# A transformer kernel on one core: setup ahead of the branch, mask passes over half their columns, and a new order of stages

## The chip, the core and the metric

The kernel runs on one core of a Trainium2 chip. Its engines are PE (matrix products; PEld is its weight load), DVE (vector), ACT (activations), POOL (general) and SP, which here only issues DMAs. Each engine runs its own list of instructions in order and waits on semaphores that the others raise. The metric is the device time of one execution in microseconds (us). Matmul results go to PSUM banks, which the program calls Q0 to Q3, HID0, HID1, Y0 and Y1.

## The reference

```python
# x: (32, 512, 256) f32; all matrices f32
x = x + linear_attention(layernorm(x))   # causal, 16 heads of 16, phi(v) = elu(v) + 1, out by W_out
x = x + ffn(layernorm(x))                # relu(h @ tern(W1).T + b1) @ tern(W2).T + b2, 256 -> 1024 -> 256
x = x + window_attention(layernorm(x))   # 16 query heads, 4 key heads, RMS-normed q and k, rotary, gain,
                                         # window of 64 keys, pairs of heads mixed, out by Wo
x = x + ffn(layernorm(x))
# tern(W) = clip(round(W / (mean|W| + 1e-5)), -1, 1)
```

Every one of the 32 sequences goes through all four parts; only the weights are shared.

## The kernel before

The products that need more than one pass's precision are split into a high and a low part (names in `_h`, `_l`, `hi`, `lo`), and each product is then three passes, or two for the FFN, whose weights are -1, 0 or 1.

**Steps.** `steps` runs 34 steps in software pipelining. `phase1` of a step works on the linear attention of sequence a, `phase2` on the window attention of the sequence before it, b. The eight blocks `up(0)` to `up(7)` and `down(0)` to `down(7)` of the FFNs are spread between the attention's stages, so that PE has work while DVE and ACT prepare the attention's next operands. Step numbers 2 to 30 are a hardware loop; the others are written out. The order of the stages is a list of calls written by hand, one list for each engine and phase: for instance, PE's `turn_q(t)` waits for DVE's `stack_lo(t)`, and DVE's `low(k)` for ACT's `relu(k)`.

**First phase**, on four chunks of 128 tokens: `qk`, `values` (projections), `phi` and `by_parity` on DVE (feature map; two copies of q with every second head zero), `turn_keys`, `state` (PE sums k v per chunk into Q2, DVE's `state` writes the running sum to SBUF, and PE's next `state` waits for that), `scores`, `mask` (DVE multiplies by the causal table), `numer`, `turn_numer`, `normalise`, `turn_y`, `y_hi`, `y_lo`, `project`, `residual`.

**Second phase**, on four tiles of 128 tokens: `sums` (sums of squares), `root_step(group, n)` (ten small dependent steps of an inverse root; group 0 is tile 0, group 1 tiles 1 to 3), `cosines`, POOL's `sines`, `rotate`, `norm_qk`, ACT's `stack_hi`, DVE's `stack_lo`, then `turn_q`, `turn_k` and their evacuation by ACT, `scores(t)`, ACT's `exps(t)`, `numer`, `turn_numer`, `normalise`, `turn_y`, `project`, `residual`. `own_apply` and `own_norm` are the layernorm of the next FFN, `next_stats`, `next_apply`, `next_norm` that of the next attention, whose input DMA SP issues after the store that waits for `finish_second`.

**Masks of the window attention.** `scores(t)` first writes the mask into the score banks: a matmul of 32 rows, of `qodd_rows` (or `qfirst_rows`) as weights and the one-hot table `hot` as moving operand, adds -1e30 where a key may not be seen. The table is one-hot over 64 queries, so it takes two passes, m = 0 and 1, each with 32 queries' rows, and each runs over the columns of all 64 queries. The four row groups g run side by side on the array. A score matmul then adds q k.

**Setup.** `both_ways` reads one flag and branches to one of two copies of the program; with these inputs the copy without guarding maxima runs. Everything that follows it, the setup of the weights too, stands inside the copies. SP alone has no branch. DVE's `prepare_rest` mixes Wo, sums |W1| and |W2| (`gsum`, then PE's `sum_rows`, then the thresholds `thr`), makes the low parts of three weights and some tables; POOL's `quantise` turns W1 and W2 into their ternary form from `thr` on.

Of the kernel before, what the change touches and what calls it, by code (L numbers as in the profile page):

```python
# [19 lines left out]
ALU = mybir.AluOpType  # L20
# [6 lines left out]
P = 128  # L27
# [68 lines left out]
def build(nc, x, w_qkv, w_out, w_b, wo_b, gain, mix, w1, b1, w2, b2, const, out):  # L96
    with ExitStack() as ctx:
# [164 lines left out]
        class Step:  # L262
# [3 lines left out]
            def __init__(self, i):  # L266
# [3 lines left out]
                self.last = isinstance(i, int) and i == NSEQ + 1  # L270

# [33 lines left out]
        def _(sp):  # L305
            sp.dma_start(gains[:, 0:H], gain.partition_broadcast(P)).then_inc(gain_in, 16)
            sp.dma_start(st_a[:, 0:KB * 3 * D].rearrange("p (k n) -> p k n", k=KB),
                         w_qkv.rearrange("(k p) n -> p k n", p=P)).then_inc(loaded_first, 16)
            sp.dma_start(cst[:], const).then_inc(loaded_first, 16)

# [7 lines left out]
            load(0)  # L318
            sp.wait_ge(x_in, 16)
# [44 lines left out]
        def _(pe):  # L364
# [163 lines left out]
            def program(guarded):  # L528
                def phase1(s):
# [137 lines left out]
                    down(4)  # L667
                    qk(a, 2)
                    values(0)
                    up(6)  # L670
                    qk(a, 3)
                    down(5)
                    up(7)
                    turn_keys(0)
                    values(1)
# [4 lines left out]
                    scores(0)  # L680
                    state(1)
                    down(7)
                    up(0)
                    numer(0, 0)
                    state(2)
                    numer(0, 1)
                    up(1)
                    turn_numer(0)
                    bias()
                    scores(1)  # L690
                    up(2)
                    turn_y(0)
# [15 lines left out]
                    up(3)  # L708
                    turn_y(2)
                    down(2)  # L710
# [8 lines left out]
                    project(3)  # L719
                    qkv(s.b, 2, a + 1)  # L720
                    down(3)
                    qkv(s.b, 3, a + 1)

                def phase2(s):
# [63 lines left out]
                    def mask(bl, g, m, blocks=1):  # L788
                        n, at_col = blocks * REP, bl % 2 * REP * W
                        table = qodd_rows if bl else qfirst_rows  # L790
                        pe.matmul(B_SCORES[g][:, at_col:at_col + n * W].rearrange("p (u q) -> p u q", u=n),  # L791
                                  table[rows_of(g), m, :], hot[rows_of(g), m, :].unsqueeze(1).broadcast_to([BR, n, W]),
# [105 lines left out]
                    own_norm(0)  # L898
                    turn_q(1)
                    turn_numer(0)  # L900
# [14 lines left out]
                    down(0)  # L915
                    turn_y(1)
                    up(2)
                    project(1)
                    turn_q(3)
                    turn_k(3)  # L920
                    numer(2)
                    down(1)
                    next_norm(0)
                    scores(3)
                    turn_numer(2)
                    next_norm(1)
                    down(2)
                    turn_y(2)
                    numer(3)
                    qk(s.next_a, 0, b)  # L930
                    project(2)
                    up(3)
# [978 lines left out]
```

## Time and profile before

| | |
|---|---|
| median of 3 executions | 2942.03 us |
| lowest and highest | 2939.92 and 2947.65 us |
| the profiled execution | 2938.5 us, of which 2936.7 us span |
| mean granted TensorE clock | 0.99 |
| PE, DVE, ACT, POOL busy | 94%, 78%, 59%, 17% |

The span runs from the first to the last instruction of the program. "Busy" is the time in which an engine has an instruction in it; matmuls overlap, and each shows its own latency too, so the distance of two starts tells the pace, and not the duration. A bracket behind a row of the timeline tells how long the engine was idle before it and what ended that. A row of the timeline or chain with x4 merges four instructions.

### The profile page before, as it was taken

To read this page: it belongs to the slowest core of one execution; us is meant where nothing else is said; L and a number is where in the kernel's file an instruction comes from. 1 tells how busy PE (TensorE), PEld (TensorE's weight loads), DVE (VectorE), ACT (ScalarE), POOL (GpSimd) and SP (SyncE) were. 2 spreads that over 40 slices of the span, in tenths; PEclk is the share of its full clock that TensorE was granted. 3 is DMA by queue.
4 is the path that set the end of the run, shared out by engine and by line. 5 is a ranking of instruction groups with operands and counts; after the bars stand their busy time and mean duration, and the time that the engine had idled before them with its cause. 6 is when DMAs were issued, how large, how long until landed. Compare 5 with 4: busy or idle time off the path is not lost.

```text
span 2936.7 us, 75526 instructions
## 1 busy us (share of the span) xinstructions
PE 2765.1 (94%) x25924; PEld 2241.4 (76%) x25924; DVE 2290.2 (78%) x5983; ACT 1744.2 (59%) x3589; POOL 486.6 (17%) x1047
## 2 busy tenths in 40 slices
PE   5799999999999999999999999999999999999986
PEld 3677777877778877778877778877778877778865
DVE  6677888787888787888787888787888787888754
ACT  2356665566665566665566665566665566665554
POOL 5111111111111111111111111111111111111110
PEclk9999999999999999999999999999999999999998
DMA  2000000000000000000000000000000000000000
GB/s 71 8 11 18 17 17 3 14 17 17 17 17 3 14 17 17 17 17 3 14 17 17 17 17 3 14 17 17 17 17 3 14 17 17 17 17 3 16 11 18
DMA packets 42050, 45.04 MB, mean 15 GB/s; under 512 B 2640, under 2 KB 41360, under 8 KB 42000
## 3 DMA queue, kind: packets, MB, share of 16 engines
q1 hardware_dynamic: 42000, 44.40, 4.8%
q8 instruction: 28, 0.46, 0.1%
q14 instruction: 22, 0.18, 0.0%
HBM read 21.32 MB, written 16.78 MB: 13 GB/s over the span
## 4 chain that ended last, share of the span: by engine, by line
PE 72%; DVE 14%; issue 7%; ACT 6%; DMA 1%; DVEq 1%; SPq 0%; POOL 0%; ACTq 0%; POOLq 0%
PE Q L380 18%; PE HID L440 13%; PE Y L464 12%; PE Q L621 5%; PE Q L594 4%; ACT a_qz L1164 4%; PE HID L388 3%; PE Q L854 2%; PE Q L644 2%; PE Q L609 2%; PE Q L791 2%; PE Q L797 2%; PE Q L867 1%; PE Q L651 1%; DVE b_ss L1564 1%
## 5 line engine op out<-in xcount | busy, mean ns | idle before, releaser
L983 ACT ACTIVATE f_r<-HID,b1c 128x512 f32<-128x512 f32 x512 | 358.3, 700 | 454.7 <-PE HID L440 433.7
L464 PE MATMUL Y<-w2t,f_hh 128*128 128x256 f32 x2048 | 539.7, 296 | 7.8 <-DVE f_hl L1328 7.8
L464 PE MATMUL Y<-w2t,f_hl 128*128 128x256 f32 x2048 | 510.9, 282 | 0.0
L440 PE MATMUL HID<-ff_xh,w1t 128*128 128x512 f32 x1024 | 433.5, 423 | 17.5 <-ACT f_hh L984 15.4
L1328 DVE TENSOR_TENSOR f_hl<-f_r,f_hh 128x512 fp32r<-128x512 f32 x512 | 351.8, 687 | 104.3 <-ACT f_hh L984 101.3
L464 PEld LDWEIGHTS Y<-w2t,f_hh 128*128 128x128 f32 x2048 | 388.8, 190 | 38.0 <-DVE f_hl L1328 13.8
L440 PE MATMUL HID<-ff_xl,w1t 128*128 128x512 f32 x1024 | 407.3, 398 | 0.0
L464 PEld LDWEIGHTS Y<-w2t,f_hl 128*128 128x128 f32 x2048 | 390.0, 190 | 6.9
L984 ACT ACTIVATE f_hh<-HID,b1c 128x512 fp32r<-128x512 f32 x512 | 356.9, 697 | 0.0
L440 PEld LDWEIGHTS HID<-ff_xh,w1t 128*128 128x128 f32 x1024 | 193.7, 189 | 99.7 <-ACT f_hh L984 44.5
L1434 DVE TENSOR_TENSOR a_s<-Q,cst 128x512 f32<-128x512 f32 x384 | 246.3, 683 | 27.8 <-PE Q L594 27.7
L1164 ACT ACTIVATE a_qz<-Q 128x512 f32<-128x512 f32 x384 | 201.7, 600 | 76.0 <-PE Q L797 76.0
L440 PEld LDWEIGHTS HID<-ff_xl,w1t 128*128 128x128 f32 x1024 | 194.6, 190 | 24.1
L1841 POOL TENSOR_TENSOR a_s<-a_s,cst 128x160 f32<-128x160 f32 x128 | 64.5, 504 | 788.4 <-ACT a_s L1019 697.6
L1820 POOL TENSOR_SCALAR at_tmp<-at_mv 128x4 f32<-128x4 f32 x64 | 20.8, 326 | 945.6 <-DVE at_mv L1306 945.6
L1072 ACT ACTIVATE a_relu<-Q 128x512 f32<-128x512 f32 x128 | 76.6, 598 | 164.8 <-PE Q L621 164.8
L594 PE MATMUL Q<-a_qz,a_kT 32*128 32x256 f32 x1536 | 152.9, 398 | 1.8 <-DVE a_qz L1425 1.8
L1320 DVE TENSOR_TENSOR at_xl<-HID,at_xh 128x512 fp32r<-128x512 f32 x122 | 84.1, 689 | 90.2 <-ACT at_xh L968 90.2
L1078 ACT ACTIVATE a_yh<-Q 128x256 fp32r<-128x256 f32 x128 | 49.2, 384 | 173.0 <-PE Q L651 173.0
L621 PE MATMUL Q<-a_s,a_v 128*32 128x128 f32 x4096 | 145.5, 276 | 3.1 <-DVE a_s L1434 3.1
L594 PE MATMUL HID<-a_qz,a_kT 32*128 32x256 f32 x512 | 145.0, 402 | 0.0
L621 PEld LDWEIGHTS Q<-a_s,a_v 128*32 128x32 f32 x4096 | 100.2, 109 | 34.0 <-issue 10.9
(197 smaller groups left out, 7366.9 us busy)
## 6 DMA issues: line engine op xcount, KB each, us to landing
x<-in_x SPq DMA_DIRECT2D x32, 512.0 KB, 4.1
out<-x SPq DMA_DIRECT2D x32, 512.0 KB, 3.0
b_vm<-b_v SPq DMA_DIRECT2D x64, 96.0 KB, 2.1
x<-in_w SPq DMA_DIRECT2D x2, 512.0 KB, 4.5
a_s<-in_w_qkv SPq DMA_DIRECT2D x1, 768.0 KB, 5.2
cst<-in_const SPq DMA_DIRECT2D x1, 645.0 KB, 6.3
ff_xn<-in_w SPq DMA_DIRECT2D x1, 512.0 KB, 6.5
f_r<-in_w SPq DMA_DIRECT2D x1, 512.0 KB, 6.8
```

Source lines behind the costliest of these rows:

```text
L380: mm = pe.matmul(dst, a, b, start=(start and k == 0 and j == 0), stop=(last and k == n - 1 and j == 2), skip_group_check=loose)
L388: mm = pe.transpose(bank[:, k * D + t * P:k * D + (t + 1) * P], n.xn[:, 2 * hf + t, k * P:(k + 1) * P], ident)
L440: mm = pe.matmul(banks[fb % 2][:], w1t[:, k, fb * P:(fb + 1) * P], src[:, k, :], start=(k == 0 and j == 0), stop=(k == KB - 1 and j == 1))
L464: mm = pe.matmul(Y[t // 2][:, (t % 2) * D:(t % 2 + 1) * D], h[:, fb % 2, t * P:(t + 1) * P], w2t[:, fb, :], start=False, stop=(fb == FB - ...
L594: mm = pe.matmul(A_SCORES[r][:, k * 2 * P:(k + 1) * 2 * P].rearrange("p (e q) -> p e q", e=2), a_kT[rows, k, ch * P:(ch + 1) * P], a_qz[ro ...
L621: mm = pe.matmul(Q[3][VW * j:VW * (j + 1), cols], a_v[:, ch, k * HB + 2 * r + e, :], a_s[:, ch % 2, r, j * P:(j + 1) * P], start=(r == 0), ...
L983: act.activation(f_r[:, fb % 2, :], banks[fb % 2][:], ACT.Relu, bias=b1c[:, fb:fb + 1]).then_inc(f_rr, 1)
L984: act.activation(f_hh[:, fb % 2, :], banks[fb % 2][:], ACT.Relu, bias=b1c[:, fb:fb + 1]).then_inc(f_act, 1)
L1164: act.activation(b_p[:, g, :], B_SCORES[g][:, :], ACT.Exp).then_inc(b_ex, 1)
L1320: dve.tensor_tensor(n.xl[:, :, hf * D:(hf + 1) * D], banks[hf][:, :].rearrange("p (k n) -> p k n", k=KB), n.xh[:, :, hf * D:(hf + 1) * D], ...
L1328: dve.tensor_tensor(f_hl[:, fb % 2, :], f_r[:, fb % 2, :], f_hh[:, fb % 2, :], ALU.subtract).then_inc(f_lo, 1)
L1434: dve.tensor_tensor(a_s[:, ch % 2, r, :].rearrange("p (h q) -> p h q", h=4), A_SCORES[r][:, :].rearrange("p (h q) -> p h q", h=4), causal. ...
```

## The change

Four things change together.

- SP loads x ahead of the constants and the weights of the projection. ACT's rounding of those weights (`round_first`), DVE's first statistics and layernorm, and POOL's first `norm_rstd` stand ahead of `both_ways`.
- DVE's `prepare_rest` is taken apart into `mix_weights`, `weight_sums(j)`, `low_weights`, `thresholds` and `small_tables`. The first two (`weight_sums` for W1) stay ahead of the steps, the others stand between the stages of step 0's first phase; PE's `sum_rows` moves there too.
- A mask pass m writes only the columns of its own 32 queries: half as many columns in each matmul, and as many matmuls as before.
- Stages of both phases stand in another order on PE, ACT and DVE.

The diff, with indentation taken off; lines of "..." stand for unchanged code.

```diff
+    self.first = isinstance(i, int) and i == 0
 def first_turn(s):
...
     sp.dma_start(gains[:, 0:H], gain.partition_broadcast(P)).then_inc(gain_in, 16)
-    sp.dma_start(st_a[:, 0:KB * 3 * D].rearrange("p (k n) -> p k n", k=KB),
-                 w_qkv.rearrange("(k p) n -> p k n", p=P)).then_inc(loaded_first, 16)
-    sp.dma_start(cst[:], const).then_inc(loaded_first, 16)
-
     def load(a):
         if needed(a * NT):
         sp.dma_start(x0[:], src.rearrange("(t p) d -> p t d", p=P)).then_inc(x_in, 16)
     load(0)
+    sp.dma_start(cst[:], const).then_inc(loaded_first, 16)
+    sp.dma_start(st_a[:, 0:KB * 3 * D].rearrange("p (k n) -> p k n", k=KB),
+                 w_qkv.rearrange("(k p) n -> p k n", p=P)).then_inc(loaded_first, 16)
     sp.wait_ge(x_in, 16)
     for half in range(KB):
         sp.dma_start(st_ffn[0][half], w1[half * P:(half + 1) * P]).then_inc(loaded, 16)
...
     up(5)
-    down(4)
     qk(a, 2)
     values(0)
     up(6)
+    down(4)
     qk(a, 3)
     down(5)
     up(7)
+    values(1)
     turn_keys(0)
-    values(1)
+    if s.first:
+        sum_rows()
     own_norm()
     turn_keys(1)
     down(6)
     state(0)
     scores(0)
+    up(0)
     state(1)
     down(7)
-    up(0)
+    state(2)
     numer(0, 0)
-    state(2)
     numer(0, 1)
     up(1)
     turn_numer(0)
+    scores(1)
     bias()
-    scores(1)
+    turn_y(0)
     up(2)
-    turn_y(0)
     down(0)
     project(0)
...
     up(3)
+    down(2)
     turn_y(2)
-    down(2)
     numer(3, 0)
     numer(3, 1)
     project(2)
     turn_y(3)
     qkv(s.b, 1, a + 1)
     project(3)
+    down(3)
     qkv(s.b, 2, a + 1)
-    down(3)
     qkv(s.b, 3, a + 1)
 def phase2(s):
...
         n, at_col = blocks * REP, bl % 2 * REP * W
         table = qodd_rows if bl else qfirst_rows
-        pe.matmul(B_SCORES[g][:, at_col:at_col + n * W].rearrange("p (u q) -> p u q", u=n),
-                  table[rows_of(g), m, :], hot[rows_of(g), m, :].unsqueeze(1).broadcast_to([BR, n, W]),
+        mine = slice(BR * m, BR * m + BR)
+        pe.matmul(B_SCORES[g][:, at_col:at_col + n * W].rearrange("p (u q) -> p u q", u=n)[:, :, mine],
+                  table[rows_of(g), m, :], hot[rows_of(g), m, mine].unsqueeze(1).broadcast_to([BR, n, BR]),
                   start=(m == 0 and (guarded or bl % 2 == 0)), stop=False, skip_group_check=True)
...
     own_norm(0)
+    turn_numer(0)
     turn_q(1)
-    turn_numer(0)
     down(7)
     turn_k(1)
     own_norm(1)
     turn_numer(1)
     scores(2)
     down(0)
+    up(2)
     turn_y(1)
-    up(2)
-    project(1)
     turn_q(3)
-    turn_k(3)
     numer(2)
     down(1)
+    turn_k(3)
+    project(1)
     next_norm(0)
     scores(3)
+    down(2)
+    next_norm(1)
     turn_numer(2)
-    next_norm(1)
-    down(2)
+    numer(3)
     turn_y(2)
-    numer(3)
     qk(s.next_a, 0, b)
     project(2)
     up(3)
...
 qk(0, 0)
 qk(0, 1)
-sum_rows()
 steps(pe, phase1, phase2)
 both_ways(pe, program)
...
     qk_exp(2)
+    relu(6)
     values(0)
-    relu(6)
     qk_exp(3)
     relu(7)
+    values(1)
     keys(0)
-    values(1)
     own_norm()
     keys(1)
     relu(0)
...
     own_norm(0)
+    evacuate_q(1)
     stack_hi(2)
-    evacuate_q(1)
     evacuate_k(1)
     own_norm(1)
     y_hi(0)
...
     relu(1)
+    exps(2)
     y_hi(1)
-    exps(2)
     relu(2)
+    evacuate_numer(2)
     evacuate_q(3)
     evacuate_k(3)
-    evacuate_numer(2)
     next_norm(0)
     exps(3)
     next_norm(1)
...
-        round_first()
-        norm_hi(at, 0, Q)
         round_rest()
         steps(act, phase1, phase2)
+    round_first()
+    norm_hi(at, 0, Q)
     both_ways(act, program)
...
                       ALU.subtract).then_inc(prepared, 1)
-def prepare_rest():
+def mix_weights():
     dve.wait_ge(loaded, 16 * N_LOADS)
     for i in range(2):
         dve.tensor_scalar(mixed[:, i, :], st_wo[:, 0, :], mixc[:, i:i + 1], None, ALU.mult).then_inc(setup, 1)
-    dve.tensor_copy(b2h[:], b2f[:]).then_inc(prepared, 1)
     dve.wait_ge(setup, 4)
     for i in range(2):
         dve.scalar_tensor_tensor(out=mixed[:, i, :], in0=st_wo[:, 1, :], scalar=mixc[:, 2 + i:3 + i],
                                  in1=mixed[:, i, :], op0=ALU.mult, op1=ALU.add).then_inc(setup, 1)
-    for j in range(2):
-        for half in range(2):
-            dve.tensor_reduce(gsum[:, 2 * j + half:2 * j + half + 1], st_ffn[j][half], X, ALU.add,
-                              apply_absolute_value=True).then_inc(abs_sums, 1)
+
+def weight_sums(j):
+
+    dve.wait_ge(loaded, 16 * N_LOADS)
+    for half in range(2):
+        dve.tensor_reduce(gsum[:, 2 * j + half:2 * j + half + 1], st_ffn[j][half], X, ALU.add,
+                          apply_absolute_value=True).then_inc(abs_sums, 1)
+
+def low_weights():
+
     dve.wait_ge(rounded, 4)
     for hi, lo, src in ((wout_h, wout_l, st_a[:, KB * 3 * D:KB * 4 * D].rearrange("p (k n) -> p k n", k=KB)),
                         (wb_h, wb_l, st_wb.rearrange("p (k n) -> p k n", k=KB)), (wob_h, wob_l, mixed)):
         dve.tensor_tensor(lo[:], src, hi[:], ALU.subtract).then_inc(prepared, 1)
+    dve.wait_ge(prepared, 5)
+
+def thresholds():
+
+    dve.wait_ge(setup_pe, 1)
+    dve.tensor_scalar(thr[:, 0:2], Y[0][:, 0:2], 1.0 / (FF * D), Q_EPS, ALU.mult, ALU.add).then_inc(setup, 1)
+    dve.wait_ge(setup, 7)
+    dve.tensor_scalar(thr[:, 2:4], thr[:, 0:2], -0.5, None, ALU.mult).then_inc(setup, 1)
+    dve.wait_ge(setup, 8)
+    dve.tensor_scalar(thr[:, 0:2], thr[:, 0:2], 0.5, None, ALU.mult).then_inc(thr_set, 1)
+
+def small_tables():
+
+    dve.wait_ge(ones_set, 5)
+    dve.tensor_copy(b2h[:], b2f[:]).then_inc(prepared, 1)
     dve.wait_ge(prepared, 6)
     dve.tensor_tensor(b2f[:], b2f[:], b2h[:], ALU.subtract).then_inc(prepared, 1)
     dve.wait_ge(prepared, 7)
...
                              in1=b2f[:].unsqueeze(1).broadcast_to([2 * BR, 2, D]),
                              op0=ALU.mult, op1=ALU.add).then_inc(prepared, 1)
-    dve.wait_ge(setup_pe, 1)
-    dve.tensor_scalar(thr[:, 0:2], Y[0][:, 0:2], 1.0 / (FF * D), Q_EPS, ALU.mult, ALU.add).then_inc(setup, 1)
-    dve.wait_ge(setup, 7)
-    dve.tensor_scalar(thr[:, 2:4], thr[:, 0:2], -0.5, None, ALU.mult).then_inc(setup, 1)
-    dve.wait_ge(setup, 8)
-    dve.tensor_scalar(thr[:, 0:2], thr[:, 0:2], 0.5, None, ALU.mult).then_inc(thr_set, 1)
-
-    dve.wait_ge(ones_set, 5)
     dve.tensor_copy(ident_b[:], ident).then_inc(prepared, 1)
     dve.tensor_copy(ident_r[:], ident).then_inc(prepared, 1)
...
     low(5)
     phi(1)
+    if s.first:
+        weight_sums(1)
+    own_apply()
     phi(2)
-    own_apply()
     low(6)
     phi(3)
     by_parity(0)
+    by_parity(1)
+    if s.first:
+        thresholds()
+        low_weights()
     low(7)
-    by_parity(1)
     own_norm_lo()
     state(0)
     mask(0)
+    if s.first:
+        small_tables()
     state(1)
     finish_first(s)
     state(2)
     next_stats()
+    normalise(0)
     low(0)
-    normalise(0)
     mask(1, (0, 1))
     y_lo(0)
     mask(1, (2, 3))
     residual(0)
+    low(1)
     next_apply()
-    low(1)
     normalise(1)
     mask(2, (0, 1))
     y_lo(1)
     mask(2, (2, 3))
     next_norm_lo(0)
     residual(1)
+    f1_stats(0)
     low(2)
     next_norm_lo(1)
     normalise(2)
     mask(3, (0, 1))
     mask(3, (2, 3))
     y_lo(2)
-    f1_stats(0)
+    low(3)
     f1_stats(1)
     residual(2)
-    low(3)
     normalise(3)
+    f1_stats(2)
+    y_lo(3)
     low(4)
-    y_lo(3)
-    f1_stats(2)
     residual(3)
     f1_stats(3)
...
         return
     sums(0)
-    cosines(0)
+    sums(1)
     root_step(0, 0)
     root_step(0, 1)
-    sums(1)
+    cosines(0)
     root_step(0, 2)
     root_step(0, 3)
     root_step(0, 4)
-    rotate(0)
+    sums(2)
     root_step(0, 5)
     root_step(0, 6)
+    sums(3)
     root_step(0, 7)
+    rotate(0)
     root_step(0, 8)
+    root_step(1, 0)
     root_step(0, 9)
+    root_step(1, 1)
     norm_qk(0)
-    sums(2)
+    root_step(1, 2)
     low(5)
     stack_lo(0)
-    sums(3)
-    root_step(1, 0)
-    root_step(1, 1)
-    root_step(1, 2)
     root_step(1, 3)
-    low(6)
     root_step(1, 4)
     cosines(1)
     if guarded:
         maxima(0)
     root_step(1, 5)
-    rotate(1)
+    low(6)
     root_step(1, 6)
     root_step(1, 7)
+    cosines(2)
     root_step(1, 8)
     if guarded:
         maxima(1)
-    cosines(2)
+    own_apply()
+    rotate(1)
     root_step(1, 9)
+    norm_qk(1)
     rotate(2)
-    norm_qk(1)
-    own_apply()
+    low(7)
     stack_lo(1)
-    low(7)
     norm_qk(2)
     own_norm_lo(0)
     normalise(0)
...
     own_norm_lo(1)
+    y_lo(0)
     stack_lo(2)
-    y_lo(0)
     cosines(3)
     rotate(3)
+    residual(0)
     norm_qk(3)
-    residual(0)
     low(0)
     next_stats()
     if guarded:
         maxima(4)
         maxima(5)
     normalise(1)
-    y_lo(1)
     stack_lo(3)
     low(1)
+    y_lo(1)
     next_apply()
     if guarded:
         maxima(6)
...
             next_norm_lo(1)
+            y_lo(2)
             f2_stats(0)
-            y_lo(2)
             residual(2)
             normalise(3)
+            low(3)
             f2_stats(1)
-            low(3)
             y_lo(3)
-            low(4)
             residual(3)
             f2_stats(2)
+            low(4)
             f2_stats(3)
-        dve.wait_ge(x_in, 16)
-        norm_stats(at, 0, x0, range(NT))
-        prepare_first()
-        norm_apply(at, 0, x0)
-        norm_lo(at, 0, Q)
-        prepare_rest()
+        mix_weights()
+        weight_sums(0)
         steps(dve, phase1, phase2)
+    dve.wait_ge(x_in, 16)
+    norm_stats(at, 0, x0, range(NT))
+    prepare_first()
+    norm_apply(at, 0, x0)
+    norm_lo(at, 0, Q)
     both_ways(dve, program)
...
             second_rstd()
-        norm_rstd(at, 0)
         quantise()
         steps(pool, phase1, phase2)
+    norm_rstd(at, 0)
     both_ways(pool, program)
```

## Rows read from the trace of the kernel before

**Rows 1.** The profile's page: busy time, share of the span and instructions of each engine

```profile
PE 2765.1 (94%) x25924; PEld 2241.4 (76%) x25924; DVE 2290.2 (78%) x5983; ACT 1744.2 (59%) x3589; POOL 486.6 (17%) x1047
```

**Rows 2.** Timeline of SP's DMA issues: start, duration (us), line, transfer

```profile
516.41 0.39 SPq L316 DMA_DIRECT2D x<-in_x  x1
604.51 0.40 SPq L316 DMA_DIRECT2D x<-in_x  x1
```

**Rows 3.** Busy time by stretch of one iteration: us, PE, PEld, DVE, ACT, POOL, clock

```profile
461.90:498.00 36.10, 35.97 (x378) 29.62 (x377) 31.06 (x78) 16.40 (x33) 3.51 (x9) 1.00 0.00 0
498.00:512.30 14.30, 12.11 (x112) 9.65 (x110) 13.62 (x45) 10.54 (x24) 5.08 (x12) 1.00 0.06 14
512.30:549.90 37.60, 37.34 (x324) 30.30 (x325) 26.14 (x66) 27.34 (x56) 5.55 (x12) 1.00 0.08 28
```

**Rows 4.** Waits of PE in that iteration (us in total, times, longest)

```profile
PE Q L754 <- DVE b_ks L1630: 1.3, 2, 0.7
PE HID L440 <- ACT f_hh L984: 0.4, 1, 0.4
```

**Rows 5.** Timeline of PE: mask passes of 256 and of 512 columns, successors

```profile
506.34 0.28 PE L791 MATMUL Q<-hot,qfirst_rows 32*128 32x256 bf16 x3
506.46 0.27 PE L791 MATMUL Q<-hot,qodd_rows 32*128 32x256 bf16 x3
...
514.96 0.39 PE L791 MATMUL Q<-hot,qodd_rows 32*128 32x512 bf16 x3
515.19 0.38 PE L791 MATMUL Q<-hot,qodd_rows 32*128 32x512 bf16 x3
```

**Rows 6.** Timeline of PE: the transposes of 128 columns of turn_q(0), turn_k(0)

```profile
504.69 0.53 PE L754 MATMUL Q<-ident_r,b_qs 128*128 128x128 f32 x4 [0.71 <-DVE b_ks L1630]
505.06 0.33 PE L763 MATMUL Q<-ident_r,b_ks 128*128 128x128 f32 x2
```

**Rows 7.** Timeline of DVE, second phase, up to stack_lo(1)

```profile
498.70 0.49 DVE L1564 TENSOR_REDUCE b_ss<-a_eq 128x20 f32<-128x320 f32 x1
...
501.54 0.37 DVE L1592 TENSOR_TENSOR b_step<-b_step,b_var 128x20 f32<-128x20 f32 x1
...
504.36 0.28 DVE L1630 TENSOR_TENSOR b_ks<-a_s,b_ks 128x128 fp32r<-128x128 f32 x1
...
511.88 0.28 DVE L1630 TENSOR_TENSOR b_ks<-a_s,b_ks 128x128 fp32r<-128x128 f32 x1
```

**Rows 8.** Timeline of ACT, second phase: exps(0), relu(7); y_hi(1), exps(2)

```profile
507.52 1.57 ACT L1164 ACTIVATE a_qz<-Q 128x512 f32<-128x512 f32 x3 [1.38 <-PE Q L797]
...
510.02 0.72 ACT L984 ACTIVATE f_hh<-HID,b1c 128x512 fp32r<-128x512 f32 x1
...
523.72 0.38 ACT L1178 ACTIVATE a_yh<-Q 128x256 fp32r<-128x256 f32 x1 [1.46 <-PE Q L874]
524.00 1.57 ACT L1164 ACTIVATE a_qz<-Q 128x512 f32<-128x512 f32 x3
```

**Rows 9.** Timeline of PE, first phase: numer(0, 0), state(2), numer(0, 1)

```profile
470.18 0.65 PE L621 MATMUL Q<-a_s,a_v 128*32 128x128 f32 x16
470.75 0.73 PE L609 MATMUL Q<-a_v,a_kt 128*128 128x136 f32 x4
471.41 0.64 PE L621 MATMUL Q<-a_s,a_v 128*32 128x128 f32 x16
```

**Rows 10.** Chain that ended last, from the start: start, us, piece

```profile
2.16 7.50 DMA x<-in_x
...
15.01 7.06 DMA mixc<-in_mix
...
34.50 0.60 DVE a_kT L1418
...
47.73 0.42 DVE a_state L1444 x2
```

**Rows 11.** The branch of `both_ways`, line L298: duration in ns, start in us

```profile
L298 PEldq COMPARE_BRANCH  x1: 6322/6322/6322, 4.9 to 4.9; - x1
```

## The prediction

> **What bounds the kernel now.** I start at the page: PE is busy 94% of the span, DVE 78% [rows 1]. That is a mean over very different stretches, so the next view is the timeline of SP, whose load of x comes once in each iteration: two of them start 88.10 us apart [rows 2]. Some 31 such periods make up most of the 2936.7 us; a change of 0.1 us in an iteration is 3.1 us in the end.
>
> Inside one iteration the busy time by stretch separates three regimes [rows 3]. From 461.9 to 498.0 (first phase) PE is busy 35.97 of 36.10 us. From 498.0 to 512.3 (start of the second phase) PE has 12.11 of 14.30 us and DVE 13.62: here DVE sets the pace. From 512.3 to 549.9 PE has 37.34 of 37.60 us again. The waits agree: PE waits 1.3 us for `b_ks`, the end of `stack_lo`, in two waits (`turn_q(0)` and `turn_q(1)`), and 0.4 us once for `relu(5)` [rows 4]. Pauses under some 0.3 us between two stages don't show as idle time, since a matmul's own latency covers them; they show in the distance of starts.
>
> **Mask passes.** A pass of 512 columns starts 0.23 us before the next (514.96 to 515.19), and one of 256 columns 0.12 us (506.34 to 506.46) [rows 5]. Four row groups run together, so this is the price of the pass. After the change tiles 1 to 3 have passes of 256 columns: 3 tiles x 2 passes x (0.23 - 0.12) = 0.66 us. Tile 0 has four passes that fall to 128 columns, for which there is no row. From below: half of 0.12, which saves 4 x 0.06 = 0.24. From above, the nearest row: transposes of 128 columns, each with its weight load, start 0.37 / 4 = 0.09 us apart (504.69 to 505.06) [rows 6], which saves 4 x 0.03 = 0.12. I take 0.16, nearer to the transposes, since a weight load belongs to each mask pass too. Together 0.8 us an iteration (0.78 to 0.90), of PE's time. On the path it is less: what tile 0 saves lies ahead of `exps(0)` and ends in DVE's stretch, where I count it below. For tiles 1 to 3 I count 0.6 of 0.66.
>
> The 128-column passes are where a rule speaks against the change. The traces' transposes show a pass with its load every 0.09 us [rows 6]. The Trainium skill (TensorE: Matmul & The Clock Gate, LDWEIGHTS) says that a load takes its columns over 1.2 GHz, and that 32 rows cost as much as 128; an estimate from that page is 0.107 us a load, so that tile 0 would save next to nothing and the sum be 0.66. Row and rule differ by 0.16 us an iteration, 5 us in all; the forecast keeps its sign by either.
>
> **Second phase, DVE's stretch.** From the first `sums(0)` at 498.70 to the last instruction of `stack_lo(1)` at 511.88 DVE has no rest [rows 7]. (a) The new list puts `sums(3)` (0.4 us from start to start) and three steps of root group 1 (0.1 each, in gaps) ahead of `stack_lo(0)`. It gains by filling the gaps of dependent steps: `root_step(0, ...)` had starts 0.2 us apart where an independent successor comes after 0.1, and some six are now filled, 0.6 us. That is even, but POOL's `sines(2)` now starts later, beside the last steps of group 0: next to POOL's work the small step of L1592 took 0.37 us [rows 7], twice its sibling's. I put `stack_lo(0)`, which ended at 504.64, 0.2 us later (-0.1 to +0.6).
>
> (b) `low(7)` now stands ahead of `stack_lo(1)`, and it waits for `relu(7)`, whose second half ended at 510.74 behind `exps(0)`, which began at 507.52 [rows 8]. `exps(0)` comes 0.2 later by (a) and 0.16 to 0.2 earlier by the masks, so `relu(7)` stays. After it: `low(7)` 0.6 us, then `stack_lo(1)` 0.55, with `own_apply` (1.3 us) now done before. It ends near 512.1, as now (511.88 + 0.28 = 512.16). PE has meanwhile done `turn_numer(0)` (0.38 us), formerly behind this wait, and `low(7)` for `down(7)` is ready. So what follows comes 0.5 us earlier (0 to 0.9). `finish_second` moves with it, and so do SP's store and load of x, on which `next_stats` waits.
>
> (c) Later, `exps(2)` no longer stands behind `y_hi(1)`. It started at 524.00, right after that `y_hi` at 523.72, before which ACT was idle for 1.46 us although the scores were issued by then [rows 8]. PE's `numer(2)` therefore need no longer wait; between `scores(2)` and it, PE has two stages less (`project(1)`, `turn_k(3)` come after), and its two pauses of 0.2 us around them go. I count 0.2 us (0 to 0.5).
>
> **First phase.** `up(0)` is now ahead of `state(1)`, and `state(2)` ahead of both `numer(0, ...)`. `state(2)` needs DVE's `state(1)`, which stands behind `mask(0)` and was over shortly before PE's `state(2)` at 470.75; until then `numer(0, 0)` filled PE's time (470.18 to 470.75) [rows 9]. In the new list PE has nothing in that slot and comes to `state(2)` some 0.4 us too early. What is behind: both numers, `up(1)`, `turn_numer(0)`. One change between narrow tiles and the full array is saved (the first numer starts 0.57 us before its successor for 16 products, the second as well), 0.1 us. Loss 0.3 us (-0.1 to +0.5). The other moves (`values(1)` ahead of `turn_keys(0)`, `down(4)` after `up(6)`, `low` and `y_lo` by one place) exchange stages of which each finds its operand ready in the old trace by my reading; they cost nothing as long as `relu(6)`, which waits for `down(4)`, is not late (0.1 us to spare).
>
> Sum of an iteration: -0.6 (masks) - 0.5 (b) - 0.2 (c) + 0.3 = -1.0 us; 31 x -1.0 = -31 us.
>
> **The front.** x landed at 2.16 + 7.50 = 9.66, behind 1.4 MB of other loads; ahead of them it should land at about 5.5. The copy's code is a second wait: PE's branch instruction took 6.32 us [rows 11], and ACT and DVE, which branch too, began behind theirs. The Trainium skill (Runtime: NRT & Kernel Launch, Instruction fetch mechanics) says that a taken branch has to fetch its target; the trace agrees. With the front ahead of the branch the first projection starts some 3 us earlier, but the branch is then paid in the middle: DVE reaches it at about 17 and its code, by PE's 6.3 us, stands at 20 to 23.5. The last load, `mixc`, landed at 22.07 [rows 10] and comes up to 2 us earlier. So DVE's setup begins near 22 as before. It took from 22.1 to 34.5 until `phi(0)` [rows 10]; now 3.9 us of it (mixing, |W1|) stand ahead of `phi(0)`, and 8.4 lie between stages, where step 0 has no FFN work and DVE waited. The chain was at `state(1)` at 47.73 [rows 10]; by the new list it needs 22 + 3.9 + 1.2 (`phi`) + 2.4 (|W2|) + 1.4 (`phi`) + 1.6 (`by_parity`) + 2.9 + 2.7 (scores, first mask) + 1.9 (mask) + 4.2 (tables), less 2.3 that overlap, about 42. That is -6 us (-2 to -9). POOL gets `thr` about 1 us later; its quantising runs beside many stages, and the thresholds come before the first FFN block wants weights, so I cost this at nothing; uncovered it would be that 1 us, once.
>
> **Sum.** 31 + 6 = 37 us less. The profiled execution took 2938.5 us with a span of 2936.7; its span would be 2900. The median of the runs lies 3.5 us above the profiled run, and 2942.0 - 37 = 2905 us.
>
> **Rivals.** (1) *DVE keeps the pace.* The moves cancel each other, and what PE saves at the masks turns into waits at `turn_q`, numer and `up`. For it: DVE's full stretch [rows 3, 4]. Against it: tiles 1 to 3 lie in a stretch with PE at 37.34 of 37.60. Then only the front is left: 2942 - 6 = 2936. Chance 0.14.
>
> (2) *Slower: `stack_lo` comes late.* Place: DVE's list ahead of `turn_q(0)` and `turn_q(1)`. If the filled gaps give nothing and POOL slows four small steps, `stack_lo(0)` is 0.8 us later; `exps(0)`, `relu(7)`, `low(7)` and `stack_lo(1)` follow one to one, and (b) turns from -0.5 to +0.6. With +0.3 in the first phase and the masks' -0.6 on the path the iteration gains 0.3 at most from elsewhere and loses 0.3 to 0.8: 2942 + 31 x 0.6 - 6 = 2955. It decides from `stack_lo(0)` 0.9 us late on. Chance 0.09.
>
> (3) *The chain opens up.* (a) is no loss, (b) gives 0.9, (c) 0.4, masks 0.8, first phase even: -2.0 us an iteration, 2942 - 62 - 7 = 2873. For it: all three are possible by my reading of the rows. Against it: so many just-in-time waits seldom all fall. Chance 0.2.
>
> The forecast, -0.4 to -1.6 us an iteration, 2925 to 2886, has 0.53; 0.04 are for things not listed. The range from 2870 to 2938 takes in cases 3 and 1 and leaves out (2) and the tails. What this kernel's measurement can tell from no change is about 0.3%, 9 us. Faster by more: 0.53 + 0.2 + part of (1), 0.76; within: 0.13; slower: 0.11.
>
> **What would show it.** In the profile after: loads of x 87.1 us apart; mask rows of 32x256 and 32x128, the first 0.12 us from start to start, the second 0.06 to 0.09; PE's wait at `turn_q(0)` as now or 0.2 longer, `turn_numer(0)` ahead of `turn_q(1)`; `exps(2)` before `y_hi(1)` with no idle time above 1 us before it; a pause of PE ahead of `state(2)`; the first `state(1)` near 42. I would be wrong if `relu(7)` were later than now relative to the second phase's start, if the pause ahead of `state(2)` grew with what DVE does there, or if a branch in mid-setup cost more than 7 us.

## The result, and the profile after

The changed kernel takes 2960.72 us (median of 5 executions, 2958.08 to 2962.88) against 2942.03 (2939.92 to 2948.31): the ratio is 1.0056, with an interval of 1.004 to 1.0071. It is slower by 19 us where I forecast 37 us less, and it lies outside the range.

The page of the changed kernel shows nearly the busy times of before [rows 1]. What is new is the clock: its mean is 0.97 where it was 0.99.

```profile
PE 2768.3 (94%) x25924; PEld 2287.5 (77%) x25924; DVE 2277.3 (77%) x5983; ACT 1738.2 (59%) x3589; POOL 491.2 (17%) x1047
```

SP's loads of x, the same view as [rows 2]: an early pair, two steady ones, and the last.

```profile
254.67 0.41 SPq L313 DMA_DIRECT2D x<-in_x  x1
341.93 0.40 SPq L313 DMA_DIRECT2D x<-in_x  x1
...
608.12 0.40 SPq L313 DMA_DIRECT2D x<-in_x  x1
696.87 0.39 SPq L313 DMA_DIRECT2D x<-in_x  x1
...
2738.06 0.40 SPq L313 DMA_DIRECT2D x<-in_x  x1
```

The steady period is 88.75 us, and was 88.10. But the iteration from 254.67 to 341.93 took 87.26, 0.84 less than before: so near the forecast of -1.0, once. PE waited 1.2 us for `stack_lo(0)` in that iteration too, but no drop of the clock followed. The busy time by stretch says what sets the two apart (columns as in [rows 3], the last three being clock, DMA share, GB/s): the same instructions, and a clock of 1.00 against 0.98.

```profile
254.67:341.93 87.26, 84.11 (x811) 69.68 (x811) 70.39 (x187) 54.07 (x113) 14.35 (x32) 1.00 0.05 14
608.12:696.87 88.75, 85.59 (x811) 71.08 (x812) 70.46 (x187) 54.09 (x113) 14.31 (x32) 0.98 0.05 14
```

Inside the steady iteration the loss sits in one place. Three stretches around `turn_q(0)`:

```profile
681.20:684.60 3.40, 1.81 (x10) 1.09 (x10) 3.37 (x13) 2.48 (x6) 2.71 (x4) 1.00 0.24 58
684.75:688.10 3.35, 3.35 (x44) 3.13 (x42) 3.26 (x12) 0.87 (x2) 1.46 (x5) 0.50 0.00 0
688.20:691.60 3.40, 3.26 (x36) 2.17 (x28) 2.03 (x4) 3.12 (x7) 1.20 (x2) 1.00 0.00 0
```

The clock falls from 2.4 to 1.2 GHz for 3.4 us. It does so in each of the 27 periods from 341.93 to 2738.06, always behind `turn_q(0)`, and before the change in none of them. PE's timeline shows what went ahead and what it costs: a pause of 1.17 us for `stack_lo(0)` (0.71 in [rows 6]), and then `down(5)` at 0.21 us a matmul, where its starts were 0.12 apart before.

```profile
682.76 0.40 PE L440 MATMUL HID<-ff_xl,w1t 128*128 128x512 f32 x1
684.33 0.54 PE L756 MATMUL Q<-ident_r,b_qs 128*128 128x128 f32 x4 [1.17 <-DVE b_ks L1651]
...
685.50 0.41 PE L464 MATMUL Y<-w2t,f_hh 128*128 128x256 f32 x1
685.72 0.42 PE L464 MATMUL Y<-w2t,f_hl 128*128 128x256 f32 x1
685.93 0.41 PE L464 MATMUL Y<-w2t,f_hh 128*128 128x256 f32 x1
```

PE's waits in that iteration (answering to [rows 4]):

```profile
PE Q L756 <- DVE b_ks L1651: 1.2, 1, 1.2
PE Q L609 <- DVE a_state L1458: 0.5, 1, 0.5
PE HID L440 <- ACT f_hh L986: 0.4, 1, 0.4
PE Q L870 <- ACT a_relu L1173: 0.3, 1, 0.3
```

The wait of `turn_q(1)` is gone, as meant; the wait of `turn_q(0)` has grown, and the early `state(2)` (L609) has a new one.

### The profile page after: what moved, and what is told of

Read it like the earlier page. It is cut to its first block, busy times and chain, and to the rows that moved or that the text cites. A ratio compares the mean times of both kernels' runs of the same rounds, so it can differ in the third digit from the quotient of the medians.

```text
span 2958.9 us, 75527 instructions
## 1 busy us (share of the span) xinstructions
PE 2768.3 (94%) x25924; PEld 2287.5 (77%) x25924; DVE 2277.3 (77%) x5983; ACT 1738.2 (59%) x3589; POOL 491.2 (17%) x1047
## 4 chain that ended last, share of the span: by engine, by line
PE 75%; DVE 11%; ACT 7%; issue 6%; DVEq 0%; DMA 0%; POOL 0%; SPq 0%; ACTq 0%; POOLq 0%
PE Q L380 19%; PE HID L440 13%; PE Y L464 13%; PE Q L621 5%; PE Q L594 4%; PE Q L857 3%; ACT a_qz L1166 3%; PE HID L388 3%; DVE a_s L1448 2%; PE Q L644 2%; PE Q L800 2%; PE Q L870 2%; PE Q L756 2%; PE Q L609 2%; PE Q L651 1%
## 5 line engine op out<-in xcount | busy, mean ns | idle before, releaser
L464 PE MATMUL Y<-w2t,f_hh 128*128 128x256 f32 x2048 | 552.6, 301 | 9.0 <-DVE f_hl L1342 9.0
L464 PE MATMUL Y<-w2t,f_hl 128*128 128x256 f32 x2048 | 528.3, 289 | 0.0
L440 PE MATMUL HID<-ff_xh,w1t 128*128 128x512 f32 x1024 | 434.2, 424 | 20.5 <-ACT f_hh L986 14.7
L464 PEld LDWEIGHTS Y<-w2t,f_hh 128*128 128x128 f32 x2048 | 402.3, 196 | 45.7 <-DVE f_hl L1342 14.7
L464 PEld LDWEIGHTS Y<-w2t,f_hl 128*128 128x128 f32 x2048 | 404.6, 198 | 9.7
L1842 POOL TENSOR_SCALAR at_tmp<-at_mv 128x4 f32<-128x4 f32 x64 | 12.9, 201 | 921.1 <-DVE at_mv L1320 921.1
L594 PE MATMUL Q<-a_qz,a_kT 32*128 32x256 f32 x1536 | 146.8, 403 | 0.0
L1686 DVE TENSOR_TENSOR x<-Q,x 128x256 f32<-128x256 f32 x128 | 54.4, 425 | 107.4 <-PE Q L380 81.2
L1842 POOL TENSOR_SCALAR ff_tmp<-ff_mv 128x4 f32<-128x4 f32 x64 | 26.4, 413 | 602.3 <-DVE ff_mv L1320 599.6
```

The costliest lines, as they stand in the source:

```text
L440: mm = pe.matmul(banks[fb % 2][:], w1t[:, k, fb * P:(fb + 1) * P], src[:, k, :], start=(k == 0 and j == 0), stop=(k == KB - 1 and j == 1))
L464: mm = pe.matmul(Y[t // 2][:, (t % 2) * D:(t % 2 + 1) * D], h[:, fb % 2, t * P:(t + 1) * P], w2t[:, fb, :], start=False, stop=(fb == FB - ...
L594: mm = pe.matmul(A_SCORES[r][:, k * 2 * P:(k + 1) * 2 * P].rearrange("p (e q) -> p e q", e=2), a_kT[rows, k, ch * P:(ch + 1) * P], a_qz[ro ...
```

## The experiments

Theory A: PE's longer pause ahead of `turn_q(0)` makes the clock fall. Theory B: the array has less to do (narrower masks), and that makes it fall. The interval of a ratio is given with it; the periods are those of the profiled executions.

**k2_head_only**: the kernel before, with DVE's new order up to `stack_lo(0)`.

```diff
 sums(0)
-cosines(0)
+sums(1)
...
+sums(2)
+sums(3)
+rotate(0)
+root_step(1, 0)
+root_step(1, 1)
+root_step(1, 2)
 low(5)
 stack_lo(0)
```

> The kernel before with one part of the change: DVE's list at the head of the second phase, up to stack_lo(0), in the new order (sums(2), sums(3) and three steps of root group 1 ahead of stack_lo(0)). Theory A (the pause): the TensorE clock falls to half for 3.4 us in each iteration because PE pauses 1.2 us for stack_lo(0), where it paused 0.7 before. Then the drop appears here too, with the old masks and the old order everywhere else: stack_lo(0) 0.45 us later and 1.3 us of half clock, the period 88.1 -> 89.5 to 89.9, time 2985 to 2998. Theory B (the array's load): the clock falls because the narrower mask passes give the array less to do. Then no drop here, only the later stack_lo(0): period 88.5, time 2955.

Measured: 2966.39 us, ratio 1.0095 (1.007 to 1.0121). Periods of 88.3 us, and in nearly every third one a drop of the clock: 88.2, 88.2, 89.7. PE's longest wait for `b_ks` was 1.2 us. The drops come without any change of the masks, so B falls. A is right in kind; that a drop comes in each iteration was not.

**k3_old_head**: the changed kernel with the old order up to `stack_lo(0)`, the same lines turned round.

> The changed kernel with DVE's old order up to stack_lo(0); sums(3) and the steps of root group 1 follow it, as before. Theory A: the pause of PE ahead of turn_q(0) is 0.7 us again, no drop in any steady iteration, period 88.75 - 1.3 - 0.45 = 87.0 (up to 87.3 if stack_lo(1) comes later), time 2910 to 2920. Theory B: the drops stay, period 88.3 or more, time near 2950.

Measured: 2930.37 us, 0.9954 (0.9938 to 0.9969); no drop in the loop, wait 0.7 us, as A says. But the period is 87.76, not 87.0: with `stack_lo(0)` on time, `turn_numer(0)` (L870) now waits 0.8 us for ACT, and the time is 10 us above what A gave.

**k4_filled**: the changed kernel with work of no use in the pause.

```diff
 def turn_q(t):
+    if t == 0:
+        pe.wait_ge(a_out, a_done * NT)
+        for _ in range(10):
+            pe.matmul(turn_bank(0, 0)[:, 0:2 * P], wout_h[:, 0, 0:P], wqkv_h[:, 0, 0:2 * P],
+                      start=True, stop=True, skip_group_check=True)
     pe.wait_ge(b_lo, b * NT + t + 1)
```

> The changed kernel, with ten matmuls of 256 columns that compute nothing put ahead of PE's wait for stack_lo(0), written to the bank that turn_q(0) then overwrites; all else, stack_lo(0)'s lateness too, as in the changed kernel. Theory A: the pause is filled (ten by 0.117 = 1.17 us), so the clock stays up and the period falls to 88.75 - 1.35 = 87.4, time 2920 to 2925. Theory B, or a clock that follows useful work: the drops stay, period 88.75 or slightly more, time 2960 to 2965.

Measured: 2916.21 us, 0.9925 (0.99 to 0.995). This settles it: `stack_lo(0)` is as late as in the changed kernel (it ends 76.15 us behind the load of x, there 76.11 to 76.16), every useful instruction is the same, and the period is 87.27. PE's timeline, and the clock over one period:

```profile
671.31 1.34 PE L751 MATMUL Q<-wqkv_h,wout_h 128*128 128x256 f32 x10
672.64 0.54 PE L761 MATMUL Q<-ident_r,b_qs 128*128 128x128 f32 x4
```

```profile
596.50:683.70 87.20, 85.22 (x821) 70.90 (x821) 70.44 (x187) 54.06 (x113) 14.31 (x32) 1.00 0.05 14
```

**k9_four_fillers**: the same with `range(4)`.

> The changed kernel with four matmuls of nothing instead of ten (0.47 us) ahead of the wait for stack_lo(0): a pause of about 0.7 us is left, as in the kernel before. Theory A in its strong form (0.7 us is harmless, 1.2 us is not): no drops, period 87.27, time 2916 to 2920. Rival: the clock follows the mean work around the pause, which is less here than in the kernel before (narrower masks), and some iterations drop: period 87.6 to 88.7.

Measured: 2915.11 us, 0.9903 (0.9876 to 0.9929), period 87.25, no drop in the loop. A pause of 0.71 us is left (the bracket), and it does no harm. PE's pause of 0.4 us for `relu(5)`, some 2.4 us ahead of `turn_q(0)`, is in all these kernels. Whether the drop goes by the length of the one pause or by the idle time of both together, the runs don't tell.

```profile
671.83 0.63 PE L751 MATMUL Q<-wqkv_h,wout_h 128*128 128x256 f32 x4
673.16 0.55 PE L761 MATMUL Q<-ident_r,b_qs 128*128 128x128 f32 x4 [0.71 <-DVE b_ks L1656]
```

**k5_old_masks**: the changed kernel with the mask passes of before.

```diff
-mine = slice(BR * m, BR * m + BR)
-... [:, :, mine], table[rows_of(g), m, :], hot[rows_of(g), m, mine] ...
+... , table[rows_of(g), m, :], hot[rows_of(g), m, :] ...
```

> The changed kernel with the old mask passes over all 64 queries' columns. Theory A: the pause of 1.2 us stays and with it the drop; the masks' columns come back, period 88.75 + 0.7 = 89.4, time near 2980. Theory B: the drop is gone, period 88.75 - 1.35 + 0.7 = 88.1, time 2942.

Measured: 2962.72 us, 1.0073 (1.005 to 1.0096). Periods of 87.98 and 89.47, mostly in turn: PE waits 1.2 us for `stack_lo(0)` in both, and the clock falls in one of the two.

```profile
527.28:615.26 87.98, 84.93 (x811) 69.89 (x812) 70.53 (x187) 54.10 (x113) 14.32 (x32) 1.00 0.05 14
615.26:704.73 89.47, 86.41 (x811) 71.14 (x812) 70.52 (x187) 54.08 (x113) 14.33 (x32) 0.98 0.04 14
```

So the pause is needed for a drop and doesn't bring one each time. It also gives the masks' worth without the clock: 87.98 - 87.27 = 0.71 us.

**k1_masks**: the kernel before with the mask change alone.

> The kernel before with the mask change alone. The pair of runs with old and new masks in the changed kernel had periods without a drop of 87.98 and 87.27, a difference of 0.71 us. Theory A (the pause decides about the clock): PE's pause ahead of turn_q(0) stays at 0.7 us, no drops, period 88.08 - 0.6 to 0.7 = 87.4, time 2942 - 21 = 2921. Theory B (the narrower passes lower the clock): drops appear, period 88.5 or more, time 2955 or more.

Measured: 2937.94 us, 0.9975 (0.9961 to 0.9989), period 87.88, no drops. The clock is as A says, the gain is not: 0.2 us instead of 0.7. PE's waits show where it went, `own_norm(0)` (L388) waiting 0.5 us where it waited 0.3 before; and the lead of 0.33 us that PE had after the masks of tile 2 ended at `turn_y(1)`, which waits for DVE.

```profile
PE Q L754 <- DVE b_ks L1631: 1.3, 2, 0.7
PE HID L388 <- DVE ff_xn L1315: 0.5, 1, 0.5
```

**k10_masks_exps**: masks, and one swap on ACT.

```diff
 relu(1)
+exps(2)
 y_hi(1)
-exps(2)
```

> The kernel before with two edits: the narrower mask passes, and exps(2) ahead of y_hi(1) on ACT. With the masks alone the period was 87.88 (0.20 less), since PE's numer(2) went on waiting for exps(2); in the changed kernel the masks were worth 0.71. If exps(2) behind y_hi(1) is what held them back, the two together give 0.6 to 0.8: period 87.3 to 87.5, time 2920 to 2926. Rival: the release is the whole new order of PE's list there (up(2), turn_q(3), turn_k(3), project(1)), and the pair gives 0.2 to 0.4: period 87.7 to 87.9, time 2932 to 2937.

Measured: 2944.73 us, 1.0002 (0.9987 to 1.0017), period 88.04. The swap alone releases nothing, and the rival's 0.2 to 0.4 isn't there either: k5_old_masks and k4_filled show the masks' 0.71 together with the whole new order on all engines. That PE's `up(2)` ahead of `turn_y(1)` is what releases it is likely by the wait above, but no run has that move alone.

**k8_state_late**: k4_filled with one stage moved back.

```diff
-state(2)
 numer(0, 0)
+state(2)
 numer(0, 1)
```

> k4_filled with PE's numer(0, 0) ahead of state(2) again, as in the kernel before. If the early state(2) costs what my forecast put on it (0.3 us, and the trace of the changed kernel shows a pause of 0.5 us in front of it), the period falls from 87.27 to 86.9 to 87.0 and the time to 2905 to 2908. Rival: the lead at this place is lost again at a later wait (turn_numer(1), which waits for ACT, had 0.13 us to spare), and the period stays within 0.1 of 87.27.

Measured: 2905.76 us, 0.9871 (0.9843 to 0.9899), period 86.86: 0.41 us for the early `state(2)`.

**k11_root1_later**: k8 with the three root steps behind `stack_lo(0)`, six fillers.

> k8_state_late with the first three steps of root group 1 behind stack_lo(0) again (two of them took 0.5 us each beside POOL, where they would take 0.2), sums(2) and sums(3) staying ahead; six fillers. If those steps are what made stack_lo(0) late, it ends 0.5 to 0.8 us earlier, and the period falls from 86.86 by 0.2 to 0.5 (86.4 to 86.7), time 2893 to 2901. Rival: the steps only move, POOL slows the ones that now stand there, stack_lo(1) sets the end, period 86.8 to 87.1, time 2905 to 2912.

Measured: 2911.81 us, 0.9886 (0.986 to 0.9911), period 87.04. `turn_q(0)` came 0.25 us earlier (0.5 to 0.8 expected), `stack_lo(1)` 0.25 later, and the iteration lost 0.18: the rival holds. The new head of DVE's list is good for the iteration (87.27 us in k4_filled, 87.76 with the old head in k3_old_head, neither with drops); only its pause is not.

**k6_front_only**: the kernel before with the new front and setup alone.

> The kernel before with the new front and the new places of the setup alone; masks and order of the stages as before. Theory F1 (the front gains some us and the half clock takes them back): the first state(1) on DVE 3 to 4 us earlier than before (47.65), a stretch of 10 to 24 us at half clock after it that ends past 45, the fourth load of x by SP (147.70 before) between 146 and 151, period 88.1, time 2940 to 2946. Theory F2 (the front's gain reaches the end as I forecast): fourth load at 142, time 2936.

Measured: 2934.59 us, 0.9967 (0.9954 to 0.998), 9 us less by the medians. Its profiled execution shows none of that: the third load of x (the expectations count it as the fourth) at 154.80, where the kernel before had 147.70.

**k7_old_front_filled**: k4_filled with the old front.

> The changed kernel with the pause filled as in k4_filled, and with the old front and the old setup. What the front is worth where the iterations have no drops: k4_filled had its fourth load of x at 145.22. Theory F1: the old front puts it within 2 us of that (147.7 in the kernel before), the period stays at 87.27, time 2916 to 2919. Theory F2: the fourth load at 151, time 2922 or more.

Measured: 2919.29 us, 0.9918 (0.9888 to 0.9948), third load at 148.64: 3 us more than k4_filled, which four executions of each, over 8 to 10 us, can't tell from nothing. The gain of k6_front_only is clear of noise. The single traces scatter more: with the old front the third load lay between 147.70 and 159.10, with the new one between 145.22 and 156.72. Most of the scatter goes with the time that the clock is at half ahead of that load (seven of the traces):

| run | front | at half clock by then, us | third load of x |
|---|---|---|---|
| before | old | 20 | 147.70 |
| k2_head_only | old | 24 | 147.90 |
| k4_filled | new | 24 | 145.22 |
| k9_four_fillers | new | 24 | 145.35 |
| after | new | 41 | 152.11 |
| k1_masks | old | 51 | 159.10 |
| k6_front_only | new | 51 | 154.80 |

Between runs with the same time at half clock the new front is ahead by 2.6 and 4.3 us (these kernels differ in more than the front).

**k12_setup_filled**: k8 with matmuls of nothing in step 0.

```diff
 def state(ch):
+    if ch and s.first:
+        for _ in range((0, 9, 22)[ch]):
+            pe.matmul(Y[1][:, :], wqkv_h[:, 0, 0:P], wqkv_h[:, 0, 0:4 * P], start=True, stop=True,
+                      skip_group_check=True)
     if ch:
         pe.wait_ge(a_st, a * 3 + ch)
```

> k8_state_late with 9 and 22 matmuls of nothing (512 columns each, to a bank not in use) in step 0 ahead of PE's waits for the first and second state of DVE, where PE stood idle for 2.5 and 8.5 us of DVE's setup. Theory F1 (the half clock after the setup takes the front's gain back): the stretch at half clock that began at 35 to 37 and lasted 10 to 24 us is gone or starts after 46, residual(0) of the first sequence, at 52.5 to 55 so far, comes at 51 to 51.5, and the time is 2 to 4 us below k8_state_late, 2902 to 2904. Rival: the fillers are late themselves or the clock falls all the same, residual(0) at 53 or later, time as k8_state_late or up to 5 us more.

Measured: 2903.17 us, 0.9859 (0.9837 to 0.9881), the lowest, but not to be told from k8_state_late. Stretches of the setup in k8_state_late, and then in k12_setup_filled:

```profile
40.00:50.00 10.00, 4.96 (x40) 3.50 (x40) 5.47 (x17) 0.60 (x1) 9.72 (x4) 0.50 0.00 0
50.00:60.00 10.00, 7.47 (x74) 5.03 (x67) 5.83 (x13) 1.36 (x3) 9.72 (x5) 0.71 0.01 2
```

```profile
40.00:50.00 10.00, 6.76 (x51) 4.19 (x49) 6.19 (x19) 0.65 (x2) 9.72 (x4) 0.83 0.01 2
50.00:60.00 10.00, 7.38 (x106) 5.56 (x106) 6.96 (x16) 1.91 (x4) 9.72 (x5) 1.00 0.00 0
```

The half clock of 20.5 us shrank to 3.4 us, and `residual(0)` came at 52.04 instead of 53.82. By the third load of x, 0.4 us of the 1.8 were left: the clock fell again in step 1.

## Why the prediction was wrong

**The step that failed** is the price of the wait in (a): "I put `stack_lo(0)`, which ended at 504.64, 0.2 us later", one to one, and rival 2 likewise. The delay was 0.48 us, inside my -0.1 to +0.6: counted from the load of x, `up(6)` of k4_filled starts 0.62 us earlier than before, and `turn_k(0)`, which follows the wait, only 0.14. It cost itself and then 1.48 us of half clock (88.75 - 87.27): 27 x 1.48 = 40 us in the loop. No line of my sum and no rival had the clock in it: I put at nothing, without a reason, what a longer pause of PE does to the pace of the matmuls behind it. Rival 2 had the right place and about the right time (2955) by the wrong mechanism: it wanted 0.9 us, 0.48 was enough. The Trainium skill (TensorE: Matmul & The Clock Gate, HAM oscillation — how this bites in real kernels) describes a clock that falls again in every turn of a loop because PE waits there for a DMA; the trace agrees in kind, for a wait for DVE of 1.2 us in a PE that is busy 94%. The prediction drew on that page for its weight loads alone.

Why `stack_lo(0)` was late is in part in DVE's timeline, beside POOL's `sines`: two of the three steps of root group 1 that were to fill gaps took 0.5 us each, where the same steps took 0.20 and 0.22 before. Each ends 0.05 to 0.07 us behind the end of the POOL instruction that it overlaps.

```profile
681.81 0.49 DVE L1599 TENSOR_SCALAR b_root<-b_var 128x60 int32<-128x60 int32 x1
682.22 0.48 DVE L1645 TENSOR_TENSOR a_s<-a_s,b_rs 128x320 f32<-128x320 f32 x1
682.62 0.51 DVE L1602 TENSOR_TENSOR b_step<-b_root 128x60 f32<-128x60 f32 x1
...
683.99 0.28 DVE L1651 TENSOR_TENSOR b_ks<-a_s,b_ks 128x128 fp32r<-128x128 f32 x1
```

```profile
681.73 0.52 POOL L1863 TENSOR_TENSOR a_s<-a_s,cst 128x160 f32<-128x160 f32 x1 [3.79 <-DVE a_s L1636]
682.21 0.85 POOL L1864 TENSOR_TENSOR a_s<-a_s,cst 128x160 f32<-128x160 f32 x1
```

But before the change `sines` slowed two steps as well, of group 0: 0.37 [rows 7] and 0.43 us instead of 0.17, ending at 501.91 and 502.37, 0.04 us behind POOL's instructions. So POOL's part grew by some 0.1 us only (0.58 against 0.46). From the start of `sums(0)` to the end of `stack_lo(0)` DVE took 5.94 us before, 6.38 now, and 6.15 in k11_root1_later, which has the three steps behind it and where `sines` slowed `norm_qk(0)` and `low(5)` instead. My "that is even" for `sums(3)` and the steps was too good; what share each has is not shown. Rows of before, a slowed step of group 0 and the first steps of group 1:

```profile
501.94 0.43 DVE L1594 SCALAR_TENSOR_TENSOR b_root<-b_step,b_root 128x20 f32<-128x20 f32 x1
...
505.30 0.20 DVE L1578 TENSOR_SCALAR b_root<-b_var 128x60 int32<-128x60 int32 x1
505.53 0.22 DVE L1581 TENSOR_TENSOR b_step<-b_root 128x60 f32<-128x60 f32 x1
```

**The other terms of an iteration** are read in k4_filled, which has them without the clock. Their sum was -0.82 (-1.0 forecast). The terms are read along PE's list, as the time by which a stage starts earlier than before, counted from the load of x.
- Masks: 0.71, forecast 0.6 on the path and 0.8 in all. The four passes of tile 0 start 0.05 to 0.06 us apart, so the nearest row (0.09) was too dear as their price. From the first pass to the first score it is 0.20 us, where it was 0.37 before (506.34 to 506.71): 0.17 saved, near my 0.16 by luck, since three distances shrink by 0.06 where I had four by 0.04. My estimate of 0.107 us a load from the Trainium skill (TensorE: Matmul & The Clock Gate, LDWEIGHTS) is near the 0.09 to 0.10 us that the rows of these loads show in k4_filled; what was wrong is to take it for the distance of the passes. The rows of the fourth row group, 0.01 us behind the others, are left out here; the last row is the first score before the change:

```profile
674.32 0.23 PE L799 MATMUL Q<-hot,qfirst_rows 32*128 32x128 bf16 x3
674.38 0.22 PE L799 MATMUL Q<-hot,qodd_rows 32*128 32x128 bf16 x3
674.44 0.22 PE L799 MATMUL Q<-hot,qfirst_rows 32*128 32x128 bf16 x3
674.49 0.22 PE L799 MATMUL Q<-hot,qodd_rows 32*128 32x128 bf16 x3
674.52 0.36 PE L805 MATMUL Q<-b_qT,b_kT 32*128 32x256 f32 x3
```

```profile
506.71 0.37 PE L797 MATMUL Q<-b_qT,b_kT 32*128 32x256 f32 x3
```

- I took the masks' gain as their own. Alone it is 0.20 (k1_masks): rival 1, that waits swallow it, is right for the old order and wrong for the new one.
- (a) and (b) lie in one stretch. PE was 0.62 us ahead at `up(6)`, 0.14 at `turn_k(0)`, 0.29 behind the masks of tile 0 (0.15 of them) and 0.77 behind `turn_numer(0)`, which stands in the place of the second wait. So (b) gave 0.5, as forecast, (a) took 0.48, and the two together gave nothing, where the sum had -0.5: it took (b) in full and had no term for (a).
- (c) and the moves around it: 0.33 (0.2 forecast).
- First phase: PE was 0.87 us ahead when it began, 0.34 at `up(1)` and 0.62 at `up(6)`, a loss of 0.25 in all, 0.3 forecast. The early `state(2)` alone costs 0.41 (k8_state_late). It waits 0.50 us for DVE, as the prediction said it might:

```profile
649.74 0.73 PE L609 MATMUL Q<-a_v,a_kt 128*128 128x136 f32 x4 [0.50 <-DVE a_state L1458]
```

Together: -0.71 (masks) + 0 (a, b) - 0.33 (c) + 0.25 (first phase) = -0.79, which is the -0.82 within the 0.05 us of such readings.

**The front**: x landed at 5.55 (5.5 forecast), DVE's setup began at 20.0 (22 forecast), but the first `state(1)` stood at 43.81, 3.8 us earlier (47.65 before) and not 5.7. `small_tables` took 6.5 us between the stages (4.2 forecast): its `b2r` ran 2.79 us beside POOL's quantising, where it had taken 0.74 us in the kernel before, ahead of POOL's quantising.

```profile
34.97 1.88 DVE L1448 TENSOR_TENSOR a_s<-Q,cst 128x512 f32<-128x512 f32 x3
...
38.94 2.79 DVE L1295 SCALAR_TENSOR_TENSOR b2r<-b2h,cst,b2f 64x512 fp32r<-64x512 f32 x1
...
43.81 0.49 DVE L1458 TENSOR_TENSOR a_state<-Q,cst 128x136 f32<-128x136 f32 x2
```

PE stood idle for it, and the clock was at half from 36 to 57, so that `residual(0)` came at 54.86, where it had come at 54.85. In that one trace the front was worth nothing. By k6_front_only it is worth 9 us (6 to 14 by the interval), by k7_old_front_filled 3 us that are not clear of noise, and by the table above 2.6 to 4.3 where the clock was at half for equally long: a gain; whether it is below or above my 6 stays open.

**The sum again**, by the two traces (2958.9 - 2936.7 = 22.2 us of span): +1.8 up to the load at 341.93, +17.9 in 27 periods, +2.5 behind the last load. I had -37, so the miss is 59 us. The clock in the loop is 40 of them, and the iteration's -0.82 instead of -1.0 is 27 x 0.18 = 5. The other 14 are at the ends, where I had -10 (the front's 6 and four more periods) and measured +4.3. The changed kernel is at half clock there for 86 us and the kernel before for 57, in these two executions. Of the 14 us, some 7 show in the front: k4_filled, with the same front and 24 us at half clock ahead of the third load instead of 41, issued that load at 145.22 instead of 152.11. Why one execution spends more time at half clock there than another, and what makes the rest, stays open.

What is left open too: why the same pause brings a drop in each iteration of one kernel and in every second or third of another. A version that beats both kernels is there: k8_state_late, 2905.76 us, the changed kernel with `state(2)` put back and the pause filled.

## What to carry to other kernels

Where PE is nearly always busy, one pause is priced twice: by its length, and by the clock that may fall behind it. Here 0.7 us brought no drop, and 1.2 us brought one, which cost 1.5 us, in nearly each, every second or every third iteration, by the kernel; look at the granted clock behind every pause that an edit lengthens. A few matmuls of nothing in the pause are a quick test, and here a cure. A gain on PE between two waits is only worth what the next wait lets through: try an edit in the order in which it will run.

## What was not expected of the hardware

- The clock fell after a pause of 1.17 us in a loop with PE at 94%, in 27 of 28 iterations, stayed at half for 3.4 us each time, and didn't fall after 0.71 us.
- A small DVE step of 128 x 60 took 0.49 to 0.51 us beside POOL's `sines`, 0.2 without, and ended just behind POOL's instruction; one of 64 x 512 took 2.79 instead of 0.74 beside POOL's quantising.
- Mask passes of 32 rows by 128 columns in four row groups start 0.05 to 0.06 us apart.
- The setup's time scatters by 11 us between kernels with the same front (third load of x at 147.70 to 159.10), along with the time at half clock in it (20 to 51 us).
